# Single-row fetches of a gather: issued by one queue in place of two, for fewer tiles

## What is computed

```python
def _round(x, w, b, gamma, beta, src, dst, etype):
    h = jax.nn.relu(_bn(x, gamma, beta))          # batch norm over the nodes
    h = jnp.einsum('nd,od->no', h, w) + b         # (12500, 640)
    h3 = h.reshape(N, T, D)                       # T = 5 edge types, D = 128
    msg = h3[src, etype]                          # one row of 512 bytes for each edge
    return jax.ops.segment_sum(msg, dst, num_segments=N)
```

## Time and profile before

| | |
|---|---|
| time, median of 3 runs | 8460.24 us (8458.51 to 8467.58) |
| the profiled execution: span | 8446.8 us (13.4 us below the median) |
| round 0, gather pass | about 230 to 2,797 us |
| round 1, gather pass | about 2,960 to 5,560 us |
| busy: PE, DVE, ACT, POOL | 49%, 47%, 17%, 54% of the span |

### The profile page before, as it was taken

The page is one execution under the profiler, slowest core; times in us unless marked ns, Lnnn a source line. Parts: engine busy times, 40 slices in busy tenths (PEclk is TensorE's granted clock), DMA queues, the critical chain, the costliest instruction groups (busy, mean ns, idle before and its releaser), DMA issues. The chain is left out here.

```text
span 8446.8 us, 99538 instructions
## 1 busy us (share of the span) xinstructions
PE 4102.0 (49%) x22648; PEld 3353.5 (40%) x22648; DVE 3975.2 (47%) x7789; ACT 1426.6 (17%) x3513; POOL 4532.3 (54%) x4709
## 2 busy tenths in 40 slices
PE   7342232331023734322232104466667888888888
PEld 3232222221022423222222103345555776777777
DVE  4553333331023567555555205643333555555568
ACT  3000000000000200000000000034444444444423
POOL 4665555564056566555555306656666555555533
PEclk8666666665566766666666556776777899888989
DMA  7111111111012511111111102222223555555567
GB/s 268 46 45 41 42 42 43 42 43 30 7 46 58 190 48 44 42 42 42 43 41 41 27 11 77 79 88 91 93 91 121 171 172 171 170 169 169 171 218 233
DMA packets 467009, 761.62 MB, mean 90 GB/s; under 512 B 115518, under 2 KB 227712, under 8 KB 465698
## 3 DMA queue, kind: packets, MB, share of 16 engines
q1 hardware_dynamic: 310212, 436.97, 17.1%
q0 software_dynamic: 148032, 316.34, 13.1%
q10 hardware_dynamic: 8192, 2.11, 0.1%
HBM read 542.21 MB, written 212.75 MB: 89 GB/s over the span
## 5 line engine op out<-in xcount | busy, mean ns | idle before, releaser
L667 POOL DMA_INDIRECT edge_rows<-messages,idx_stage x1432 | 1368.4, 956 | 1059.3 <-DVE idx_stage L1043 648.2
L1756 PE MATMUL banks<-w_types,h_stage 128*128 128x512 f32 x320 | 321.5, 1107 | 1864.1 <-issue 1153.5
L667 POOL DMA_INDIRECT buf_a<-messages,idx_stage x727 | 695.7, 957 | 715.8 <-DVE idx_stage L1043 487.8
L728 POOL DMA_INDIRECT sorted_rows<-edge_rows,idx_stage x784 | 760.4, 970 | 543.3 <-DVE edge_rows L1576 329.8
L728 POOL DMA_INDIRECT sorted_rows<-buf_a,idx_stage x784 | 760.2, 970 | 538.4 <-DVE buf_a L1576 305.0
L667 POOL DMA_INDIRECT buf_x<-messages,idx_stage x727 | 696.5, 958 | 647.5 <-DVE idx_stage L1043 418.8
L1951 PE MATMUL banks<-work,buf_a 128*128 128x128 f32 x5640 | 839.6, 312 | 144.3 <-issue 98.7
L1951 PEld LDWEIGHTS banks<-work,buf_a 128*128 128x128 f32 x5640 | 798.1, 225 | 196.9 <-issue 187.2
L1756 PEld LDWEIGHTS banks<-w_types,h_stage 128*128 128x128 f32 x320 | 77.1, 299 | 1901.5 <-issue 1175.4
L1998 PE MATMUL banks<-wf,work 128*128 128x128 f32 x3136 | 616.1, 333 | 188.3 <-issue 180.3
L1998 PEld LDWEIGHTS banks<-wf,work 128*128 128x128 f32 x3136 | 487.9, 226 | 363.2 <-issue 362.5
(11 more groups left out here) (222 smaller groups left out, 7592.6 us busy)
## 6 DMA issues: line engine op xcount, KB each, us to landing
buf_a<-sorted_rows SPq DMA_DIRECT2D x705, 288.0 KB
messages<-work SPq DMA_DIRECT2D x196, 320.0 KB
buf_a<-dst_rows SPq DMA_DIRECT2D x198, 256.0 KB
first_batch<-messages SPq DMA_DIRECT2D x2048, 0.5 KB
buf_x<-messages ACTq DMA_DIRECT2D x2048, 0.5 KB
buf_x<-messages SPq DMA_DIRECT2D x2048, 0.5 KB
buf_a<-messages ACTq DMA_DIRECT2D x2048, 0.5 KB
buf_a<-messages SPq DMA_DIRECT2D x2048, 0.5 KB
```

What stands on the lines that cost most here:

```text
L667: nc.gpsimd.indirect_dma_start(gathered[p][h][:, t, :], None, source, bass.IndirectOffsetOnAxis(ap=idx_stage[:, h, t:t + 1], axis=0),).the ...
L728: nc.gpsimd.indirect_dma_start(sorted_rows, bass.IndirectOffsetOnAxis(ap=idx_stage[:, 2 * u + h, t:t + 1], axis=0), msg_halves[2 * u + h][ ...
L1756: nc.tensor.matmul(ps_raw[:, 0:WIDE], h_stage[:, t % 2, :], w_types[p][:, 0:WIDE], start=True, stop=True)
```

## The change

- The two groups at halves 132 and 134 and those at 176 and 178 are no longer fetched: `FETCHED` has 6 groups, 3 batches, 24 tiles a round in place of 40. GpSimd gathers the other 16 tiles.
- All 3 batches are issued by SyncE, 3,072 DMAs a round, each as a whole. The last batch has no late part: nothing is fetched between the chunks.
- ScalarE issues no fetch. Its waits for the table's stores go too.
- The batches after the first lie in other parts of the raw rows' buffer (`FETCH_HALF`): batch 1 where the fourth raw half was, batch 2 where the seventh was, so they may start once raw halves 4 and 7 were summed (a wait on `s_raw_agg`).
- Code for an input in which a group of edges spans more than 128 nodes (`beyond`) is changed in three places. The branch isn't taken with this input.

```diff
-FETCHED = ((112, 0), (114, 0), (132, 0), (134, 0), (148, 0), (150, 0), (176, 0), (178, 0), (184, 0), (186, 0))
+FETCHED = ((112, 0), (114, 0), (148, 0), (150, 0), (184, 0), (186, 0))
 BATCHES = len(FETCHED) // 2
-SP_BATCHES, ACT_BATCHES = (0, 2, 4), (1, 3)
-FETCH_HALF = (None, 2, 3, 5, 6)
-ACT_FIRST_RAW, ACT_UNITS = RAW_TWICE, 4
-LATE_FIRST, LATE_UNITS = {4: 80, 3: 104}, 3
+FETCH_HALF = (None, 3, 6)
...
             def fetch_batches(p):
                 sp.wait_ge(s_setup, FETCH_LINKS)
-                for i in SP_BATCHES:
+                for i in range(BATCHES):
                     if i:
                         sp.wait_ge(s_raw_agg, raw_summed(p, i))
                     if p:
                         sp.wait_ge(s_acc[0], SUMS + 2 * (FETCHED[2 * i + 1][0] - 2 * RAW_ITERS[0] + 1))
-                    for e in late_units(i, 0) if i in LATE_FIRST else range(P):
-                        fetch_rows(nc.sync, mybir.EngineType.SP, p, i, e)
-
-            def fetch_late(p, m):
-                for e in late_units(SP_BATCHES[-1], m):
-                    fetch_rows(nc.sync, mybir.EngineType.SP, p, SP_BATCHES[-1], e)
+                    for e in range(P):
+                        fetch_rows(p, i, e)
...
                         store_nodes(TURNED + m, m, y_row_stage)
-                        fetch_late(0, m + 1)
...
                 load_x(m + 1)
-                fetch_late(1, m)
                 store_chunk(m)
...
-                    if t >= ACT_FIRST_RAW:
-                        fetch_some(rnd, ACT_UNITS)
-                fetch_some(rnd, P + LATE_FIRST[ACT_BATCHES[-1]] - (RAW_TILES - ACT_FIRST_RAW) * ACT_UNITS)
...
-                    fetch_some(0, LATE_UNITS)
...
                 deviation(m)
-                fetch_some(1, LATE_UNITS)
```

More of the change, by code:

```diff
@@ L22 @@
-import itertools
 import numpy as np
@@ L389, in raw_summed, with fetch_rows @@
             return RAW_BEFORE[p] // HALF_TILES + FETCH_HALF[i] + 2
[L391 to L395, removed]
+        def fetch_rows(p, i, e):
             rows = table[p].rearrange("(o n) d -> o (n d)", o=1).bitcast(u8)
             at = nc.values_load_multi_w_load_instructions(
-                fetch_at[e:e + 1, i, :, :].rearrange("p j t -> p (j t)"), engines=[kind], min_val=0,
+                fetch_at[e:e + 1, i, :, :].rearrange("p j t -> p (j t)"), engines=[mybir.EngineType.SP], min_val=0,
                 max_val=(N * T - 1) * ROW_BYTES, skip_runtime_bounds_check_because="a source times the types plus a type, in bytes")[1]
@@ L401, in fetch_rows @@
             for t in range(HALF_TILES):
-                engine.dma_start(into[:, t * ROW_BYTES:(t + 1) * ROW_BYTES], rows[:, ds(at[t], ROW_BYTES)]
+                nc.sync.dma_start(into[:, t * ROW_BYTES:(t + 1) * ROW_BYTES], rows[:, ds(at[t], ROW_BYTES)]
                                  ).then_inc(s_fetched[i], 16)
@@ L761, in _ @@
                                      ACT.Copy).then_inc(s_node_staged, 1)
[L763 to L767, removed]
             for rnd in range(2):
@@ L786, in _ @@
                     normalised(n, n)
[L788 to L791, removed]
                 for t in range(RAW_ITERS[rnd] * ITER_TILES):
@@ L1781, in raw_beyond @@
             def raw_beyond(p):
+                pe.wait_ge(s_row_ready[p], BLOCKS + SLOT3)
                 for half in range(2 * RAW_ITERS[p]):
@@ L1953, in sum_segment, with beyond_block @@
                 last.then_inc(s_seg, 1)
-            def beyond_block(k, j, b, opening):
+            def beyond_block(k, j, b):
                 step = (k * 2 + j) * BLOCKS + b
@@ L1961, in beyond_block @@
                     tile = slice(t * P, (t + 1) * P)
-                    last = nc.tensor.matmul(ps_h[j][:, tile], x_onehot[:, 0, tile], x_h, start=opening, stop=False)
+                    last = nc.tensor.matmul(ps_h[j][:, tile], x_onehot[:, 0, tile], x_h, start=False, stop=False)
                 last.then_inc(s_xagg[2], 1)
@@ L1977, in convolution_step @@
                         if beyond:
-                            beyond_block(k, j, 0, True)
-                            with pe.Fori(1, BLOCKS) as b:
-                                beyond_block(k, j, b, False)
+                            nc.tensor.matmul(ps_h[j], ones_d[0:1, :], zero_col[0:1, :].broadcast_to([1, WIDE]), start=True, stop=False)
+                            with pe.Fori(0, BLOCKS) as b:
+                                beyond_block(k, j, b)
                         for t in range(GROUP_TILES):
@@ L1984, in convolution_step @@
                             last = nc.tensor.matmul(ps_h[j][:, tile], spread[:, h, edges], h_win[:, h, j, :],
-                                                    start=not beyond, stop=True)
+                                                    start=not beyond, stop=not beyond or t == GROUP_TILES - 1)
                         last.then_inc(s_hexp, 1)
```

## The result

| | kernel before | changed kernel |
|---|---|---|
| time, median us | 8463.91 (8458.51 to 8490.47, 4 runs) | 8780.77 (8764.09 to 8787.62, 4 runs) |
| ratio | 1 | 1.0365, 95% interval 1.0344 to 1.0386 |
| span of the profiled execution | 8446.8 us | 8785.5 us |

3.65% slower; 8,737 us had been forecast, in a range of 8,560 to 8,860. I call them the long and the short pace, and compare the times of kernels only within a session. The profiles of before and after are both of the long pace.

The account below looks back on a forecast made before the run. SP's list of single-row fetches ahead of round 0's store and round 1's load was taken as the bound: 8446.8 + 264 (longer list) + 13 (tails) = 8,724, with 13.4 from span to median 8,737 us; range 8,560 to 8,860.

Parts of the forecast that it names:

- GpSimd's pace: Gathers through the raw tiles: 0.608 to 0.6625 tiles a us once ScalarE fetches none, worth nothing by itself.
- ScalarE's leaving: SP's queue: ScalarE's fetches hardly change SP's pace, so their going would not speed SP.
- The list's term: SP's queue ahead of store and load: 2,688 fetches become 3,072, +146 us in round 0, +118 in round 1.
- pace next to gathers: SP's issue while GpSimd gathers: 1.065 fetches a us in round 0, 1.1275 in round 1.
- The bound that the prediction called high: SP's list: each tile costs 2.01 fetches, 1.90 in round 1; list +170 and +173, time 8,827 us.
- The tails: After the standstills: 8 more GpSimd tiles a round, +24, less 11 for the late batch's wait; together +13 us.
- wait of tens of us at half 184: TensorE's 23 us wait for the late batch would vanish, worth -11 us.
- TensorE would no longer wait for ScalarE's L797: Raw tiles: TensorE's 711 us wait, put down to ScalarE's fetches, would no longer be the longest of L1756.
- rival C: Raw tiles held by something other than ScalarE's fetches; GpSimd stays at 0.608, time 8,737 to 8,877 us; 8%.
- A: SP's queue beside gathers: freed by ScalarE's leaving, faster; no change at about 1.27 a us, 8,273 us at 1.4; 7%.
- D: A mixture: SP's pace rises part of the way towards 1.27 a us, time 8,480 to 8,564 us; 4%.
- B: SP's queue beside dense gathers: slower still, 0.93 a us, rounds +241 and +259, time 8,973 us; 7%.

Follow-up runs that it names:

- e1_late_b: The changed kernel with 48 partitions of the last batch fetched late between the chunks again, 2,688 fetches ahead of the store; 8,487 us, 0.999 of the kernel before.
- e2_whole_b: The kernel before with only SP's last batch issued whole, 3,072 fetches a round, ScalarE's batches kept; 8,803 us, 1.0371 of the kernel before.
- e4_none_b: The changed kernel with no row fetched singly, GpSimd gathering all 1,483 tiles a round; 7,620 us, 0.898 of the kernel before.
- a2_after: The changed kernel itself, timed again in a later session; 6,317 us beside 6,271 of the kernel before, 1.0073.

## Why the prediction was right, and where its sizes were off

**The mechanism** was right in the main: SP's list is the bound, the 384 fetches that moved ahead of the store and the load are the loss (e1_late_b takes all of it away, e2_whole_b has all of it), GpSimd's pace is hidden behind the list, and ScalarE's leaving gives SP nothing. At the short pace none of this is the bound, which the prediction didn't know of and gave no chance.

**The list's term was too small:** +146 and +118 forecast, +166.5 and +170.0 measured. The step that failed is the pace next to gathers, 1.065 and 1.1275, read over the first 400 us of each round. That stretch is not like the rest: later in the passes SP issued 1.003 and 1.022, and in the changed kernel too its first 400 us were faster (432 in 397.32 us, 1.087). GpSimd's density doesn't explain it, since it was 0.6625 tiles a us then and 0.676 and 0.663 later; why SP is faster at the start of a pass stays open.

The bound that the prediction called high, a fixed number of fetches lost for each tile, solved from the whole of before (2.01 and 1.90 a tile), gave +170 and +173 and was the better law. Solved in the same way from the whole of the changed kernel, it is (2.355 x 2,290.2 - 3,072) / 1,162 = 2.00 and (2.303 x 2,266.5 - 3,072) / 1,136 = 1.89, nearly the same. The expectations used 1.97 and 1.93, which is what the changed kernel shows between 700 and 1,750 us and between 3,600 and 4,600 us, and met e1_late_b's 2,115.3 with 2,113. Nor does ScalarE change it: with its fetches (2.303 - 1.141) / 0.608 = 1.91 a tile, without them (2.303 - 1.022) / 0.663 = 1.93. Between 1,210 and 1,840 us the trace shows where the tiles take it: SP issued 486 in the 529 us in which GpSimd went from gather to gather (0.92 a us), and 143 in the 100 us of GpSimd's pauses (1.43).

**Some of the closeness is luck.** The two list terms were 72.5 us short in sum (264 for 336.5). Everything else between the spans was taken at +13 and came to +2.2, and the 13.4 us by which the median of before lay above its span were added, where the median of the changed kernel lay 4.7 below its span. So the median was missed by 44 us and the span by some 61.

**The tails** were taken at +13 in sum and came to -15.6 in round 0 and some +7 in round 1, inside the bounds of -32 and +24. No wait of tens of us at half 184 is left, as said.

**ScalarE and GpSimd.** GpSimd's pace rose from 0.608 to 0.663 in round 1, as forecast (0.6625), and was worth nothing by itself. But that TensorE would no longer wait for ScalarE's L797 (now L772) was wrong. The waits over the whole span of the changed kernel:

```profile
ACT h_stage L772 <- remote: 2599.8, 120, 51.8
...
PE banks L1726 <- ACT h_stage L772: 1472.9, 130, 25.8
```

1,473 us in place of 711, with ScalarE issuing no fetch. So rival C had a part of the truth: the raw tiles are held by something else too. In e4_none_b, where SP fetches nothing either, the same wait is 746 us. One raw tile of the changed kernel in the timelines of PE, ACT, DVE and POOL shows the order of events:

```profile
1005.61 0.30 PE L1722 MATMUL banks<-ident,buf_x 128*128 128x128 f32 x1 [1.24 <-issue]
...
1020.62 0.46 ACT L772 ACTIVATE h_stage<-banks,bn_shift,bn_scale 128x128 f32<-128x128 f32 x1 [23.49 <-remote]
...
1020.69 0.29 DVE L1136 TENSOR_TENSOR buf_a<-buf_a,banks 128x128 f32 x1 [10.77 <-remote]
...
1016.93 0.95 POOL L652 DMA_INDIRECT edge_rows<-messages,idx_stage  x1 [0.30 <-issue]
1021.82 0.95 POOL L652 DMA_INDIRECT buf_x<-messages,idx_stage  x1 [3.93 <-DVE idx_stage L1013]
```

TensorE turned the tile at 1,005.6; ScalarE, which had nothing else to do, took it up at 1,020.6, and VectorE woke at the same moment, some 3 us after the last gather of GpSimd's run (1,016.9 to 1,017.9). Between 800 and 1,100 us 11 of ScalarE's 13 raw tiles start like this, 1.7 to 5.2 us after the end of a run of gathers, and so do all 13 between 3,600 and 3,900 us. At the short pace ScalarE's answer is there at once, with gathers going on: TensorE's transform waited 0.55 us for it. At the long pace, then, ScalarE's and VectorE's dependent steps mostly come when GpSimd pauses. That its gathers are what holds them fits the order, since GpSimd stops first, but no run took the gathers away to test it.

**The rivals.** A and D, the faster ones, are out: without ScalarE's fetches SP's pace was no higher, and the 1.27 a us that A wanted was exceeded at the short pace alone, which is another matter. (A's 1.14 a us for ScalarE was no reading: beside SP's 877 in 770 us ScalarE issued 971, 1.26 a us.) In pace the truth lay between the forecast (1.065 and 1.1275) and B (0.93), at 1.003 and 1.022. C's price is out, since GpSimd's pace did rise. The Trainium skill's rule that starting DMAs on several engines saves only a usually small time ("DMA: Bandwidth & Descriptors", section "Issuing engines are not separate DMA queues") is about the usual case, and the long pace is not that case: the time of SP's issuing is the bound there. At the short pace no run compares one issuing engine with two alone; the whole change costs 0.7% there.

## What to carry to other kernels

A queue that issues single small DMAs is a worker with a list: count its issues ahead of each duty that others wait for, and price them by its measured pace there, as so much for each of the other engine's DMAs that fall into the stretch, not as one rate read at the start. Moving work off an engine pays only up to the next list; here not fetching at all (0.898) beat both kernels at the long pace, and lost 1.4% at the short one. Where a kernel's time can have two values, an optimum found at one of them has to be timed at the other.

## What the runs showed of the hardware that was not expected

**Two paces of one chip.** In one session the kernel before took 6,271 us, in a later one on the same chip 8,617, in the next on another chip 8,496, in the last on the first chip 6,271 again; runs of one kernel within a session agree within 1%. The line of SP's fetches by duration (min, median, max ns), first of the changed kernel at the long pace, then of a2_after at the short one:

```profile
L393 SPq MOVE first_batch<-messages x2048: 2/29/1409, 229.5 to 4070.8; - x187
...
L393 SPq MOVE first_batch<-messages x2048: 29/29/38, 187.1 to 2588.5; - x187
```

MOVE is a register instruction that goes with each fetch, not a transfer. Its median is 29 ns at both paces, but of the 6,144 that go with fetches 1,000 took over 35 ns at the long pace, up to 1,409, and 2 at the short one, 38 at most. So SP's own instructions are held too, whatever holds them. GpSimd's gather takes 0.95 us at both, and one follows the other after 0.30 us at both; its pace falls from 0.79 to 0.67 tiles a us by the pauses in which it waits for VectorE's indices. What GpSimd does is thus the same, and what the others can do beside it is not. What puts a chip at one pace or the other, the runs don't show.

**GpSimd's gathers slow SP's issue, at the long pace alone.** At the short pace SP issued 2.35 fetches a us beside gathers, at the long one 1.0 beside them and 2.35 without. The Trainium skill ("DMA: Bandwidth & Descriptors", section "SWDGE vs HWDGE vs iDMA") calls DMAs issued from SP or ScalarE immune to one interference, VectorE's locking GpSimd out of the memory to which it writes descriptors. What slows SP here is another one, which comes with GpSimd's gathers; the immunity doesn't cover it, and by what path it works the runs don't show.
